# Graph attention: outputs taken through DRAM in pairs, another order of the DMA queue, and a quotient on GpSimd

## What is computed

```python
h = maximum(layernorm(x), 0)                       # x: 64 x 128 x 384
q, k, v = h @ Wq + bq, h @ Wk + bk, h @ Wv + bv     # 12 heads of 32
scores = q @ k.T / sqrt(32) + beta * adj
scores = where(adj > 0, scores, -9e15)             # adj: 64 x 128 x 128
out = x + softmax(scores) @ v
```

## Time and profile before

| | |
|---|---|
| median of 3 runs | 545.62 us (545.51 to 547.7) |
| profiled execution, its time | 551.03 us |
| its span, first to last instruction | 548.9 us |
| TensorE matmuls busy | 507.4 us (92%) |
| VectorE busy | 467.3 us (85%) |
| ScalarE busy | 443.0 us (81%) |
| GpSimd busy | 127.0 us (23%) |
| mean granted clock of TensorE | 0.987 |

### The profile page before, as it was taken

The page is one execution under the profiler, slowest core; times in us unless marked ns, Lnnn a source line. Parts: engine busy times, 40 slices in busy tenths (PEclk is TensorE's granted clock), DMA queues, the critical chain, the costliest instruction groups (busy, mean ns, idle before and its releaser), DMA issues.

```text
span 548.9 us, 17414 instructions
## 1 busy us (share of the span) xinstructions
PE 507.4 (92%) x5142; PEld 418.8 (76%) x5142; DVE 467.3 (85%) x2323; ACT 443.0 (81%) x1816; POOL 127.0 (23%) x204
## 2 busy tenths in 40 slices
PE   8897989997999989899899989999898998999986
PEld 7676868776878778688787878778786887888774
DVE  5686878978989798898989989898898998887796
ACT  3568596796988969788796988889698897989885
POOL 5412121222222222221222222122222221111121
PEclk9999999999999999999999999999899999999999
DMA  7516466776776777767687776767668566655311
GB/s 244 169 55 197 127 209 204 214 218 204 222 244 180 242 215 220 222 202 217 203 249 217 223 233 211 227 206 242 203 192 252 178 198 201 179 160 161 94 45 59
DMA packets 132840, 106.20 MB, mean 193 GB/s; under 512 B 44464, under 2 KB 121904, under 8 KB 132784
## 3 DMA queue, kind: packets, MB, share of 16 engines
q1 hardware_dynamic: 132784, 105.57, 63.5%
HBM read 55.84 MB, written 49.68 MB: 192 GB/s over the span
## 4 chain that ended last, share of the span: by engine, by line
SPq 38%; PE 19%; DMA 12%; DVE 10%; issue 8%; ACT 3%; DVEq 0%; ACTq 0%
SPq L425 12%; SPq L402 11%; DMA out_rows<-out_blocks 8%; PE G_ps L892 7%; PE S_ps L961 4%; SPq L429 4%; SPq L443 4%; PE S_ps L913 4%; SPq L394 4%; DMA probs_moved<-probs_rows 4%; DVE probs L726 4%; PE PT_ps L945 2%; PE PT_ps L929 2%; ACT probs_blocks L542 2%; SPq L419 1%
## 5 line engine op out<-in xcount | busy, mean ns | idle before, releaser
L527 ACT ACTIVATE probs<-probs,negmax 128x128 f32<-128x128 f32 x532 | 206.0, 397 | 0.0
L726 DVE CUSTOM_DVE_ANT_0 probs<-S_ps,bias 128x128 f32<-128x128 f32 x768 | 165.8, 284 | 14.4 <-PE S_ps L913 14.4
L542 ACT ACTIVATE probs_blocks<-probs,negmax 128x128 f32<-128x128 f32 x236 | 91.9, 393 | 71.9 <-DVE negmax L726 71.8
L498 POOL TENSOR_TENSOR y<-y,x_ring 128x384 f32<-128x384 f32 x63 | 63.9, 1014 | 299.6 <-DVE y L744 299.6
L892 PE MATMUL G_ps<-h_hi,w_hi 128*128 128x512 f32 x288 | 120.1, 417 | 0.0
L892 PE MATMUL G_ps<-h_hi,w_lo 128*128 128x512 f32 x288 | 119.0, 413 | 0.0
L892 PE MATMUL G_ps<-h_lo,w_hi 128*128 128x512 f32 x288 | 117.6, 408 | 0.0
L527 ACT ACTIVATION_READ_ACCUMULATOR probs<-probs,negmax 128x1 f32 x532 | 105.0, 197 | 0.0
L764 DVE STREAM_TRANSPOSE probsT<-probs_moved 128x512 f32<-128x512 f32 x59 | 41.8, 709 | 43.3 <-DMA probs_moved<-probs_rows 43.2
L913 PEld LDWEIGHTS S_ps<-qk 32*128 32x128 f32 x1536 | 50.9, 188 | 33.8 <-issue 32.3
L929 PE MATMUL PT_ps<-probsT,v 128*32 128x128 f32 x1512 | 55.6, 281 | 22.1 <-DVE probsT L764 10.7
(11 more groups left out here) (60 smaller groups left out, 724.7 us busy)
## 6 DMA issues: line engine op xcount, KB each, us to landing
probs_rows<-probs_blocks SPq DMA_DIRECT2D x59, 256.0 KB, 2.8
probs_moved<-probs_rows SPq DMA_DIRECT2D x236, 64.0 KB, 2.3
out_dram<-y SPq DMA_DIRECT2D x63, 192.0 KB, 2.0
x_ring<-in_x_dram SPq DMA_DIRECT2D x61, 192.0 KB, 3.0
out_rows<-out_blocks SPq DMA_DIRECT2D x58, 192.0 KB, 2.1
out_moved<-out_rows SPq DMA_DIRECT2D x232, 48.0 KB, 2.1
xhat_rows<-xhat_blocks SPq DMA_DIRECT2D x26, 384.0 KB, 2.7
xhat_moved<-xhat_rows SPq DMA_DIRECT2D x104, 96.0 KB, 2.5
```

The source lines that it names most:

```text
L498: nc.gpsimd.tensor_tensor(y[:, z.s % 2 ^ d, :], y[:, z.s % 2 ^ d, :], x_ring[:, bass.ds(at, D)], ALU.add).then_inc(y_ready, 1)
L527: last = nc.scalar.activation(p, p, ACT.Exp, bias=negmax[:, e, j * KC + m:j * KC + m + 1], scale=TURN, accum_out=rowsum[:, e, m * HC + j:m ...
L542: last = nc.scalar.activation(blocks[:, j, :, :], probs[:, a, j, 0, :].rearrange("p (c e) -> p c e", c=HC), ACT.Exp, bias=negmax[:, a, j * ...
L726: last = nc.vector.tensor_tensor_reduce(probs[:, a, j, m, :], S_ps[:, j, m * N:(m + 1) * N], bias[(z.par + 1) % 2][:, z.s, :], 1.0, LARGES ...
```

## The change

- Outputs go through DRAM in pairs. `out_blocks` holds two graphs. SyncE writes both in slots 1 and 3 (after the write of xhat, before that of the probabilities) and reads them back at the end of the same slot in four DMAs of 96 KB. The rows in DRAM get 768 bytes per block instead of 384.
- A moved output is divided and added two slots after its store (`moved = [2]`) instead of one; `rinv` and `y` have four places instead of two. `y` and `out_moved` lie in the space of `w_raw`, which is free by then.
- The quotient of the moved outputs is GpSimd's, ahead of its add. VectorE keeps that of the last graphs.
- SyncE's order in a slot: read probabilities, load adj and x (`load_ahead`), write or read xhat, write the pair of outputs, write probabilities, write a result, read the pair. `LOADS` is `[[0], [1], [2, 3], []]` instead of `[[0], [1, 2], [3], []]`.

```diff
-LOADS = [[0], [1, 2], [3], []]
+LOADS = [[0], [1], [2, 3], []]
...
-        out_blocks = sb("out_blocks", [P, D])
-        out_rows = nc.dram_tensor("out_rows", [2, P, D], F32, kind="Internal").ap()
-        out_moved = sb("out_moved", [P, 2, D])
-        y = sb("y", [P, 2, D])
+        SIX = 2 * KC * HD
+        out_blocks = sb("out_blocks", [P, HC * SIX])
+        out_rows = nc.dram_tensor("out_rows", [2, P, HC * SIX], F32, kind="Internal").ap()
+
+        later = w_raw.rearrange("p k n -> p (k n)")
+        out_moved = later[:, 0:2 * HC * SIX].rearrange("p (i n) -> p i n", i=2)
+        y = later[:, 2 * HC * SIX:2 * HC * SIX + GROUP * D].rearrange("p (i n) -> p i n", i=GROUP)
...
-                before = 0 <= 4 * (n - 1) + s - 3 < FIRST_F
-                self.moved, self.turned = [1] * before, [0] * (self.F and self.O and not self.L)
+                first_f = n == NG and s == 0
+                self.moved = [2] * (not self.F and 4 * (n - 1) + s - 4 >= 0) + [2, 1] * first_f
+                self.turned = [0] * (self.F and self.O and not self.L)
...  SyncE
-                if z.W:
-
-                    sp.wait_ge(outT_stored, z.o + 1)
-                    sp.dma_start(out_rows[z.s % 2, :, :], out_blocks[:, :]).then_inc(out_rows_written, 16)
+                load_ahead(z)
...
+                if z.W and z.s % 2 == 1:
+
+                    sp.wait_ge(outT_stored, z.o + 1)
+                    sp.dma_start(out_rows[1 - z.s // 2, :, :], out_blocks[:, :]).then_inc(out_rows_written, 16)
                 if z.Q:
                     sp.wait_ge(probs_ready[0], z.a + 1)
                     sp.dma_start(probs_rows[z.s % 2, :, :], probs_blocks[:, :]).then_inc(probs_rows_written, 16)
-                if z.W:
-                    sp.wait_ge(out_rows_written, 16 * (z.o + 1))
+                for d in z.moved + z.turned:
+
+                    sp.wait_ge(y_ready, z.o + 1 - d)
+                    place = (z.s - 2 - d) % GROUP
+                    sp.dma_start(out[bass.ds(z.o - d, 1), :, :].rearrange("b t d -> t (b d)"), y[:, place, :]).then_inc(out_written[place], 16)
+                if z.W and z.s % 2 == 1:
+                    sp.wait_ge(out_rows_written, 16 * (z.pairs_written() + 1))
                     for b in range(HC):
-                        came = out_rows[z.s % 2, :, b * THREE:(b + 1) * THREE].rearrange("(j p) n -> p j n", j=HC)
-                        goes = out_moved[b * HD:(b + 1) * HD, z.s % 2, :].rearrange("p (j n) -> p j n", j=HC)
+                        came = out_rows[1 - z.s // 2, :, b * SIX:(b + 1) * SIX].rearrange("(j p) n -> p j n", j=HC)
+                        goes = out_moved[b * HD:(b + 1) * HD, 1 - z.s // 2, :].rearrange("p (j n) -> p j n", j=HC)
...  GpSimd
+            def quotient(z, d):
+
+                pool.wait_ge(rinv_ready, z.o + 1 - d)
+                back = z.s - 2 - d
+                place, half = back % GROUP, back // 2 % 2
+                pool.wait_ge(out_blocks_moved[half], 16 * HC * (z.written(d) + 1))
+                came = out_moved[:, half, :].rearrange("p (j s n) -> p s j n", j=HC, s=2)[:, z.s % 2 ^ d % 2, :, :].rearrange("p j (m d) -> p j m d", m=KC)
+
+                if started(z.written(d)):
+                    pool.wait_ge(out_written[place], 16 * z.written(d))
+                nc.gpsimd.tensor_tensor(y[:, place, :].rearrange("p (j m d) -> p j m d", j=HC, m=KC), came,
+                                        rinv[:, place, :].rearrange("p (j m) -> p j m", m=KC).unsqueeze(3).broadcast_to([P, HC, KC, HD]),
+                                        ALU.mult).then_inc(moved_normalised, 1)
...  VectorE
-                    if started(z.o):
-                        dve.wait_ge(out_rows_written, 16 * z.o)
+                    if z.s % 2 == 0 and started(z.pairs_written()):
+                        dve.wait_ge(out_rows_written, 16 * z.pairs_written())
...
-                for d in z.moved:
-                    quotient(z, d)
```

More of the change, by code:

```diff
@@ L496, in slot @@
                     at = z.ring(-1, back) if back >= 0 else z.ring(-2, GROUP + back)
-                    pool.wait_ge(normalised, z.o + 1 - d)
-                    nc.gpsimd.tensor_tensor(y[:, z.s % 2 ^ d, :], y[:, z.s % 2 ^ d, :], x_ring[:, bass.ds(at, D)], ALU.add).then_inc(y_ready, 1)
+                    if d in z.moved:
+                        quotient(z, d)
+                        pool.wait_ge(moved_normalised, z.o + 1 - d)
+                    else:
+                        pool.wait_ge(normalised, z.o + 1 - FIRST_F)
+                    place = back % GROUP
+                    nc.gpsimd.tensor_tensor(y[:, place, :], y[:, place, :], x_ring[:, bass.ds(at, D)], ALU.add).then_inc(y_ready, 1)
                 for q in z.stats:
@@ L822, in slot @@
                 if z.F and z.A:
-                    quotient(z, 0)
+                    quotient(z)
                     store_probsT(z, 1)
```

111 lines of the change are left out of this document (54 added, 57 removed).

## The result

The changed kernel takes 551.18 us (median of 6 runs, 549.7 to 553.94) where the kernel before takes 546.96 beside it (6 runs, 545.51 to 549.3). The ratio is 1.0075, 95% interval 1.0046 to 1.0104: slower by 0.75%. The forecast was 519, with a range of 511 to 533, so the time lies outside the range and on its far side.

A forecast was written before the change was run, and what follows sets the result against it. TensorE needs 29.8 us a group, but SyncE's late issues hold groups at about 32. Savings of 23.7 (groups 3 to 13), 4.9 (group 2) and 0.5 (group 1), together 29.1, gave 516.5 to 521.9, taken as 519; range 511 to 533.

The forecast's parts named there:

- 59 issues by 0.47, 49 after: SyncE's queue: a group issues 59 DMAs of some 0.47 us; pairs make it 49, 4.7 us less of the queue.
- The pair's write lands in 2.7: Odd slots: the pair's 384 KB write lands in 2.7 us, as xhat's does, not the single write's 2.1.
- d: How late SyncE is with the probabilities' write and reads: 3.05 before, 1.95 after in odd slots, 1.7 or 2.2 in even.
- the odd loop: Group length by d of the odd slots: 26.0+3.9 = 29.9 us; by the even slots 30.55; 30.3 taken.
- M+7.05: Odd slots: reads of outputs go 7.05 us after VectorE's masking starts (M); later than M+7.5 would show the prediction wrong.
- The loop: Over two slots, masking, exponentials, probabilities' write and reads, VectorE's transpose, next masking: 13.0 us plus d, 16.05 before the change.
- only move past waits that are long over: SyncE's loads, now earlier in a slot: they cost only their issues, already counted.
- nothing of its own: Taking the quotient off VectorE, 0.46 us in each slot, was given no gain, since VectorE isn't the bound.
- What a port costs: Overlap of GpSimd and VectorE in SBUF: GpSimd loses 0.26 us, hidden, VectorE nothing; bias above 0.35 us would show it wrong.
- New waits: VectorE's store of outT must find the pair's write landed, tightest in slot 0: nothing at a landing of 2.7 us.
- the slower one: Rival: reads of outputs head the queue; a pair landing of 3.95 us takes all back, 4.2 gives 551; chance 0.06.
- the path stays SyncE's: Rival: the pair's write lands in 3.3 us, a group takes about 31.5, the time is 530 to 535; chance 0.14.

The follow-up runs named there:

- no_trip: The kernel after without the pair's write, its reads and the wait for that write; GpSimd multiplies bv_rows, the attention output is left out: 518.22 us, 0.9412.
- xhat_last: loads_last with the odd slot's writes in the order pair, probabilities, xhat: 527.3 us, 0.9592 of the kernel before.
- after_vq: The kernel after with the quotient of the moved outputs back on VectorE: 551.22 us, 1.0013 of the kernel before.
- loads_last: The kernel after with the loads of adj and x back at the end of a slot: 546.2 us, 0.9939 of the kernel before.
- before_gq: The kernel before with only the quotient of the moved outputs put on GpSimd: 548.29 us, 0.9953 of the kernel before.
- before_xhat_last: The kernel before with xhat's write in odd slots moved behind the write of the probabilities: 552.09 us, 1.0057 of the kernel before.
- pair_first: The kernel after with the pair's write ahead of xhat's write in odd slots: 536.94 us, 0.9756 of the kernel before.
- xhat_last_vq: xhat_last with the quotient of the moved outputs back on VectorE: 532.64 us, 0.9697 of the kernel before.

## Why the prediction was wrong

*What bounds the kernel.* Right. TensorE needs 29.8 a group, and SyncE stands between; no_trip (29.76 a group) and xhat_last (30.93), with the clock at 1.0, show it.

*Where the 32 us are.* The profiled execution was to take 521.9 us and took 553.9. The eleven groups 3 to 13 were to take 333.3 and took 359.8 (99.38 to 459.15 us), group 2 31.3 and 37.6: 32.8 together. So the error lies in groups 2 to 13, not in the prologue or the end.

*59 issues by 0.47, 49 after.* Right, also their size (four take 1.75 to 1.79). But a freed issue is no freed time where the queue next meets a landing: of some 47 us, 41 became waits.

*The pair's write lands in 2.7, "these are also the bounds".* This is the step that failed. It was taken from xhat's write in the kernel before, of the same size, and size wasn't what decided. There xhat's stands behind one write of 192 KB (0.55 us before it in most slots) and the loads lie at the other end of the slot. The pair's stands behind xhat's 384 KB and, in slot 1, is fourth of five DMAs issued within 2.1 us. It took 3.88 and 3.24 in the group shown. The prediction's own formula (d of 1.95 at 2.7, so d = landing less 0.75) gives for their mean, 3.56, a d of 2.81 and a group of 26.0 + 5.6 = 31.6 by the odd loop and 32.3 by the even one; measured are 31.99 there, 32.11 over eight. Its sign of being wrong came too: the reads of outputs go at M+8.9 in the slot 1 shown (312.92 less 304.04, where the masking starts) and at M+7.5 in slot 3, not at M+7.05. With 2.7 and 2.8 put for the four landings of the group shown, SyncE's four slots would be 8.09, 7.89, 7.32 and 7.52, 30.8 in all. So of the 1.7 between forecast and measurement 1.2 is the landings: 1.7 longer for the pair's two, 0.5 shorter for the probabilities' two in even slots. The other 0.5 is that the prediction looked at SyncE against VectorE's masking only, and let it start each odd slot in time; the pair's write went at M+5.0 in slot 1, not M+4.35.

*The loop.* The one that closed is SyncE's own, over writes and reads, not the one through VectorE's transpose and masking. The two are close in length, and so the first could hide behind the second. They differ in what helps: faster work on VectorE can't shorten the one that closed (after_vq against the kernel after).

*The loads "only move past waits that are long over".* The waits were over, but the loads stand in front of the write of which the landing is the critical one. 5 to 6 us (loads_last).

*The quotient, "nothing of its own".* Right for this kernel (before_gq 0.5% faster, after_vq not told from the kernel after). GpSimd's took 833 ns, under the 1.1 us taken and under the lower bound of 1.0:

```profile
L504 POOL TENSOR_TENSOR w_raw<-w_raw,rinv 128x384 f32<-128x384 f32 x58 | 48.3, 833 | 162.1 <-DMA w_raw<-out_rows 96.1
```

*What a port costs.* "VectorE nothing" was wrong, see below, and the bias passed its sign of 0.35 us (357 ns in the mean), yet without weight: GpSimd's quotient gained wherever it could be seen.

*New waits.* VectorE's store of outT waited 2.7 us in total for the pair's landing, and SyncE never for a result: near enough to the forecast.

*Groups 1 and 2 and the end.* Group 2 was to fall from 36.2 to 31.3 and took 37.61; the next took 36.02. A long landing hurts most where the queue has the most to catch up. The clock was granted below full speed as before (0.95 over groups 1 and 2, 0.91 from 426.23 to 459.15 us), so "fewer waits should leave fewer" drops had no occasion; xhat_last and no_trip, with fewer waits, have 1.0 in the profiled execution.

*The rivals.* The one that came to pass is the slower one: the pair's landing at the head of the queue takes all back, from 3.95 us on, 551 us at 4.2. Its place was right. Its landing was reached in slots 1 (3.9 to 4.2) but not in slots 3 (3.0 to 3.5), so that its 551 is the measured time is in part luck. It got 0.06 because "xhat's 384 KB land in 2.7 at the same load", that is, by the same argument that sized the term. The rival "the path stays SyncE's" had its condition met to the tenth (3.3) and its price too low, since it counted a median for a wait of which every second one is 4.

## What to carry to other kernels

A queue that issues writes, waits for them and reads them back is a ring of its own: add up issues and landings around it, and compare that sum with the bound of the kernel before counting what a saved issue is worth. Take the landing of a write from a row with the same neighbours in the queue, not from one of the same size. Where the queue sets the pace, put the write that is waited for soonest first and the one with the most slack last; that also keeps a write of which the tile isn't ready from holding up those that have theirs. And a part that measures as worthless may only lie behind another bound: before_xhat_last and the kernel after are each slower than the kernel before, xhat_last, which has both their edits and the loads at the end of the slot, is 4.1% faster.

## What the runs showed of the hardware

**A landing depends on what was issued around it.** The same write of 384 KB landed in 2.3 us with nothing ahead of it but reads of 64 KB and a load (xhat_last), in 3.0 behind xhat's 384 KB (loads_last), and in 3.9 to 4.2 behind xhat's and two loads of 192 and 256 KB (slots 1 of the kernel after; 3.0 in the one slot where the loads lay 2.1 us and more ahead). The write of the probabilities took 2.0 in the odd slots of xhat_last, 1.2 us and more behind the pair's, and in the kernel after, as third of three writes within 1 us, 3.4 in slots 3 and 4.1 in slots 1 (medians). What comes behind shows as well: in pair_first's odd slots at 146.10 and 161.38 us, where xhat's write follows 0.82 us after the pair's, the pair lands in 2.3, and in the other slots 3, where it follows after 0.55, mostly in 2.5 to 2.8. So xhat_last's 2.3 may owe something to the later writes behind it too. The mean share of busy DMA engines is 0.74 in the group of the kernel before, 0.71 in that of the kernel after and 0.73 in those of xhat_last, so it isn't the load over a group that decides but the few microseconds around the issue.

**VectorE can be the one that waits at the port.** Here is a normalisation of xhat_last, which by itself takes 0.44:

```profile
204.24 1.06 DVE L686 TENSOR_SCALAR xhat_blocks<-x_ring,meanvar,rstd 128x384 f32<-128x384 f32 x1
```

```profile
204.25 0.83 POOL L505 TENSOR_TENSOR w_raw<-w_raw,rinv 128x384 f32<-128x384 f32 x1 [4.12 <-DMA w_raw<-out_rows]
```

It ends 0.22 us after GpSimd's quotient does. The two starts lie 0.01 us apart and don't show who came second, but another one, at 235.10 us, began 0.26 after its quotient, took 0.79 and also ended 0.22 behind it. Six of 52 took 0.76 to 1.07, each beside a quotient. Over the kernel the normalisation takes 500 ns in the mean in xhat_last and 442 in xhat_last_vq, 3.0 us in all. In the kernel after three groups are longer than in the kernel before: the normalisation (481 against 442), the bias (357 against 326) and the mask term (227 against 204), 5.4 us in all, by a few instructions each that stand beside a quotient or an add. The Trainium skill (SBUF — State Buffer, Who interferes with whom) says that `tensor_scalar` may run in a mode that takes the port shared with GpSimd, and that the other then blocks for the whole instruction; the trace agrees, at 235.10 us. The prediction had looked only at VectorE's instructions with two SBUF operands. Of those the bias was hit in three of 64 cases in the kernel after, up to 1.11 us, and the low part (0.59 at most) in none.
